# Memory attention of a perceiver stack on Trainium2: every probability block of a middle pair turned by VectorE and through DRAM, the second batch's transfers issued by ScalarE, and its weighting placed after the next pair's first scores

## What is computed

```python
def _L1_xattn_ref(x, memories, ln_g, ln_b, Wq, Wkv, Wm, Wo, bo):
    # HEADS = 16, DIM_HEAD = 64, INNER = 1024
    xn = (x - mu) * rsqrt(var + EPS) * ln_g + ln_b
    q = _split_heads(xn @ Wq)
    kv = xn @ Wkv
    k = _split_heads(kv[..., :INNER])
    v = _split_heads(kv[..., INNER:])
    mem = _split_heads(memories @ Wm)
    k = jnp.concatenate([k, mem], axis=2)
    v = jnp.concatenate([v, mem], axis=2)
    dots = jnp.einsum('bhid,bhjd->bhij', q, k) * DIM_HEAD ** (-0.5)
    attn = jax.nn.softmax(dots, axis=-1)
    out = jnp.einsum('bhij,bhjd->bhid', attn, v)
    return out.transpose(0, 2, 1, 3).reshape(b, n, h * d) @ Wo + bo
```

## Time and profile before

| | us |
|---|---|
| median of three runs | 2071.55 |
| range | 2068.11 to 2072.27 |
| the profiled execution's own time | 2070.35 |
| its span in the trace | 2068.6 |

### The profile page before, as it was taken

One profiled execution on the slowest core, in us unless ns is written; L12 is line 12 of the kernel. 1 busy time (PEld: TensorE's weight loads), 2 busy tenths in 40 slices (PEclk: granted clock), 3 DMA queues, 4 the chain that ended last, 5 costly groups with the idle time before them and its releaser, 6 DMA issues. The chain is left out here.

```text
span 2068.6 us, 34656 instructions
## 1 busy us (share of the span) xinstructions
PE 1985.6 (96%) x14206; PEld 1441.4 (70%) x14206; DVE 1229.0 (59%) x2068; ACT 882.2 (43%) x2075; POOL 61.1 (3%) x78
## 2 busy tenths in 40 slices
PE   7999999899999999989999999899999999989999
PEld 6864455578878888844446788677777777774687
DVE  6446589563356888899999310355444453548563
ACT  4224443353324323589997332233232332333342
POOL 0000000000000000200000000000000000000122
PEclk9999999999999999999999999899999999999999
DMA  7210000131110110120002145566567464643001
GB/s 267 82 49 1 1 2 2 42 107 41 41 42 21 62 42 25 58 102 1 21 1 94 52 139 166 169 181 172 130 185 187 116 191 126 160 159 100 1 1 41
DMA packets 125581, 174.73 MB, mean 84 GB/s; under 512 B 12256, under 2 KB 83936, under 8 KB 124960
## 3 DMA queue, kind: packets, MB, share of 16 engines
q1 hardware_dynamic: 125424, 172.52, 27.9%
HBM read 118.09 MB, written 22.94 MB: 68 GB/s over the span
## 5 line engine op out<-in xcount | busy, mean ns | idle before, releaser
L1307 ACT ACTIVATE R<-bank 128x512 f32<-128x512 f32 (+1 forms) x150 | 89.4, 599 | 393.2 <-PE bank L965 292.2
L1576 ACT ACTIVATE R<-R 128x64 f32<-128x64 f32 x896 | 217.0, 342 | 3.4 <-DVE R L2288 3.4
L962 PE MATMUL bank<-cth,wmh 128*128 128x512 f32 x512 | 207.4, 405 | 5.5 <-ACT arena L1681 4.2
L962 PE MATMUL bank<-cth,wml 128*128 128x512 f32 x512 | 200.7, 392 | 0.0
L532 PE MATMUL bank<-XN,arena 128*128 128x512 f32 x320 | 148.6, 617 | 0.0
L965 PE MATMUL bank<-ctl,wmh 128*128 128x512 f32 x512 | 137.8, 391 | 0.0
L962 PEld LDWEIGHTS bank<-cth,wmh 128*128 128x128 f32 x512 | 96.7, 189 | 39.3 <-issue 19.1
L532 PE MATMUL bank<-Y,arena 128*128 128x512 f32 x256 | 115.9, 597 | 1.7 <-ACT H L1619 1.7
L532 PEld LDWEIGHTS bank<-XN,arena 128*128 128x128 f32 x320 | 61.4, 198 | 72.1 <-issue 71.7
L965 PEld LDWEIGHTS bank<-ctl,wmh 128*128 128x128 f32 x512 | 96.6, 189 | 20.6
L962 PEld LDWEIGHTS bank<-cth,wml 128*128 128x128 f32 x512 | 96.8, 189 | 18.2
(11 more groups left out here) (442 smaller groups left out, 4173.9 us busy)
## 6 DMA issues: line engine op xcount, KB each, us to landing
Y<-value_turn SPq DMA_DIRECT2D x240, 128.0 KB, 2.9
H<-in_ctxT SPq DMA_DIRECT2D x30, 512.0 KB, 5.3
arena<-in_L_attn_mlp_w SPq DMA_DIRECT2D x8, 1024.0 KB, 5.2
probs<-R SPq DMA_DIRECT2D x15, 512.0 KB, 4.0
R<-probs SPq DMA_DIRECT2D x60, 128.0 KB, 3.1
R<-value_rows SPq DMA_DIRECT2D x32, 132.0 KB
arena<-in_L_ffn_Wg SPq DMA_DIRECT2D x4, 1024.0 KB, 6.7
arena<-in_L_ffn_Wu SPq DMA_DIRECT2D x4, 1024.0 KB, 5.3
```

The lines of the kernel that those rows point to most:

```text
L962: mm(bank, w_[:, o // 4, k, tl(o % 4)], cth[:, k, :, :], start=(k == 0 and w_ is wmh), stop=False)
L1307: fn(dst, src, ACT.Copy).then_inc(act_bank_free, 1)
L1576: last = fn(into[:, x // 2, h, :, x % 2], RC["Ey"][:, t, h, :], ACT.Copy, scale=RC["Ex"][:, t, h, 8 * j + x:8 * j + x + 1])
```

## The change

Pair 0 joins the last pair (`at_edge`): its values and probabilities go by TensorE alone, without transfers. In pairs 1 to 14 both batches' probabilities are turned by VectorE and sent through DRAM; b1 has its own DRAM buffer and semaphores, and its one transfer out and four back are issued by ScalarE among its copies. Unit 4 of the memories goes to a VectorE bank, as 2 and 3 do. `weighted(b1)` is issued by TensorE after the next pair's first scores, and VectorE scales its result after those scores' maxima. SyncE issues b0's four transfers back before the last four value transfers. The second scores come after units 2 and 3, and units 0 and 1 after them and unit 4.

```diff
+BY_DVE = (2, 3, 4)
...
+        def at_edge(pr):
+            return pr in (0, PAIRS - 1)
...
-                    b = open_dve(("mem", pr, o)) if o in (2, 3) else open_act(("mem", pr, o))
+                    b = open_dve(("mem", pr, o)) if o in BY_DVE else open_act(("mem", pr, o))
...
                 attention_scores(b0)
-                if pr == PAIRS - 1:
+                if pr:
+                    weighted(b0 - 1)
+                if at_edge(pr):
                     value_blocks(b0)
-                fill(2)
+                fill(2, 3)
+                attention_scores(b1)
+                if at_edge(pr):
+                    value_blocks(b1)
+                fill(4)
                 fill(0, 1)
                 if pr:
                     out_rows(pr - 1)
-                attention_scores(b1)
-                if pr == PAIRS - 1:
-                    value_blocks(b1)
-                fill(3)
                 if pr and pr % (CB // 2) == 0:
                     on_act(("ot", pr - 1))
                     output(pr // (CB // 2) - 1)
-                if pr == PAIRS - 1:
+                if at_edge(pr):
                     prob_blocks(b0)
-                fill(4)
-                prob_blocks(b1)
                 fill(5)
+                if at_edge(pr):
+                    prob_blocks(b1)
+                fill(6)
                 if pr == PAIRS - 1:
                     token_rows(4, 0)
                 prob_tail(pr)
-                fill(6, 7)
+                fill(7)
                 weighted(b0)
-                weighted(b1)
+            weighted(2 * PAIRS - 1)
...
                 exponentials(b0)
-                fill(0, 1)
+                exponentials(b1)
+                fill(0)
+                if not at_edge(pr):
+                    act.wait_ge(probs_turned[1], 2 * pr)
+                    if pr > 1:
+                        act.wait_ge(probs_full[1], 64 * (pr - 1))
+                    act.dma_start(dram["probs"][1].rearrange("c k j n -> (c k) (j n)"), prob_turn[1].rearrange("p j b n -> p (j b n)")
+                                  ).then_inc(probs_spilled[1], 16)
+                fill(1)
                 if pr:
                     out_rows(pr - 1)
-                exponentials(b1)
-                fill(4, 5, 6, 7)
+                fill(5)
+                if not at_edge(pr):
+                    act.wait_ge(probs_spilled[1], 16 * pr)
+                    for j in range(4):
+                        act.dma_start(probs_moved[1][32 * j:32 * j + 32].rearrange("p c b n -> p c (b n)"),
+                                      dram["probs"][1][:, :, j, :].rearrange("c k n -> k c n")).then_inc(probs_full[1], 16)
+                fill(6, 7)
...
                 maxima(b0)
-                if pr and pr + 1 < PAIRS:
-                    memory(pr + 1, (2,))
-                if pr < PAIRS - 1:
+                if pr:
+                    weighted(b0 - 1)
+                if at_edge(pr):
...
+                    values(b0)
+                else:
                     turn_values(pr)
-                    turn_probs(pr)
+                    memory(pr + 1)
+                maxima(b1)
+                if at_edge(pr):
+                    values(b1)
                 else:
...
-                maxima(b1)
-                if pr == PAIRS - 1:
-                    values(b1)
-                if pr and pr + 1 < PAIRS:
-                    memory(pr + 1, (3,))
+                    turn_probs(b0)
+                if pr + 1 < PAIRS:
+                    memory(pr + 1, (4,))
+                if not at_edge(pr):
+                    turn_probs(b1)
...
                 for a in range(4):
-                    if a == 2 and pr < PAIRS - 1:
...
+                    if a == 2:
+                        spill_probs(0)
+                    if a == 3:
+                        sp.wait_ge(probs_spilled[0], 16 * pr)
+                        for j in range(4):
+                            sp.dma_start(probs_moved[0][32 * j:32 * j + 32].rearrange("p c b n -> p c (b n)"),
+                                         dram["probs"][0][:, :, j, :].rearrange("c k n -> k c n")).then_inc(probs_full[0], 16)
                     for b in range(4):
                         sp.dma_start(RD["vt"][32 * b:32 * b + 32, :, a, :], value_turn[32 * a:32 * a + 32, :, b, :]
                                      ).then_inc(values_full, 16)
```

More of the change, by code:

```diff
@@ L247, in perceiver @@
         values_turned, values_full = sem("values_turned"), sem("values_full")
-        probs_turned, probs_spilled, probs_full = sem("probs_turned"), sem("probs_spilled"), sem("probs_full")
+        probs_turned, probs_spilled, probs_full = ([sem(f"{n_}{i}") for i in range(2)]
+                                                   for n_ in ("probs_turned", "probs_spilled", "probs_full"))
         k_full = [sem(f"k_full{i}") for i in range(2)]
@@ L390, in perceiver @@
         prob_turn = R[:, 14912:15936].rearrange("p (j b n) -> p j b n", j=4, b=2)
-        probs_moved = RD["pt"][:, 0:2, :].rearrange("p b n -> p (b n)").rearrange("p (c b n) -> p c b n", c=4, b=2)
+        two_moved = RD["pt"].rearrange("p (i b) n -> p i (b n)", i=2)
+        probs_moved = [two_moved[:, i].rearrange("p (c b n) -> p c b n", c=4, b=2) for i in range(2)]
+        prob_turn = [prob_turn, two_moved[:, 1].rearrange("p (j b n) -> p j b n", j=4, b=2)]
+        def at_edge(pr):
+            return pr in (0, PAIRS - 1)
         RDa = region([("p", (4, 612)), ("k", (2, 8, 64))], base=arena[:, 2:4, :, :].rearrange("p s a b -> p (s a b)"), limit=4096)
@@ L1070, in part @@
                     return last
-                if i == 0 and bb // 2 < PAIRS - 1:
-                    pe.wait_ge(values_full, 256 * (bb // 2 + 1))
-                if i == 0 and bb // 2 < PAIRS - 1:
-                    pe.wait_ge(probs_full, 64 * (bb // 2 + 1))
+                if not at_edge(bb // 2):
+                    pe.wait_ge(values_full, 256 * (bb // 2))
+                    pe.wait_ge(probs_full[i], 64 * (bb // 2))
                 for blk in range(2):
-                    if i:
-                        part(lambda g, c: RD["pt"][:, 2 + blk, 128 * g + 32 * c:128 * g + 32 * c + 32], RD["vt"][:, 2 + blk], blk == 0, None, False)
-                    else:
-                        part(lambda g, c: probs_moved[:, c, blk, 32 * g:32 * g + 32], RD["vt"][:, blk], blk == 0, None, False)
+                    part(lambda g, c: probs_moved[i][:, c, blk, 32 * g:32 * g + 32], RD["vt"][:, 2 * i + blk], blk == 0, None, False)
                 if i == 0:
@@ L1719, in _ @@
                     split_high(1)
-            memory(1, [o for o in EARLY if o not in (2, 3)])
+            memory(1, [o for o in EARLY if o not in BY_DVE])
             for pr in range(PAIRS):
```

71 lines of the change are left out of this document (33 added, 38 removed).

## The result

| kernel | median, us | range, us | runs |
|---|---|---|---|
| before | 2071.3 | 2065.96 to 2073.91 | 13 |
| after | 2082.82 | 2072.92 to 2085.98 | 13 |

The ratio is 1.0054 with a 95% interval of 1.0042 to 1.0066. The forecast was 2057 us with a range of 2049 to 2069, so time and sign are both wrong. Each ratio in this document is to launches of before made beside that kernel's own, and their medians lay between 2068.6 and 2071.3 us; where two kernels are a few us apart, read their ratios as well as their medians. The profiled execution of after took 2078.71 us; its span is 2076.9.

The account below looks back on a forecast made before the run. TensorE was taken as the bound. Pairs 0 to 14: 18.5 + 11 x 30.52 + 3 x 45.29 + 1.6 = 491.7 us against 507.07; 15.4 saved, less 1.0 in pair 15, gave 2057 us, range 2049 to 2069.

Parts of the forecast that it names:

- Pair 0: First pair, made without transfers: its weighting starts 18.5 us after the pair's start, where the pair took 29.46 us before.
- Rival 2: Pair 0 stays at half clock, so scores and a unit take 3.6 us more: 2061 us; chance 0.10.
- ScalarE's issues at nothing: ScalarE's five DMA issues of 0.5 us among its copies are covered by TensorE's work and cost nothing.
- Rival 3: ScalarE's issues and waits outrun their cover, unit 7 is emptied late and pairs grow; 2084 us at L = 2; chance 0.08.
- The chain to unit 0: Middle pairs: splits, maxima, turning, copies and first exponential hold TensorE 1.17 us before unit 0; the pair takes 30.41 us.
- Output pairs: Three pairs with output projection: 30.41 + 13.98 us plus a 0.90 us wait before `output` for ScalarE's copy, 45.29 us.
- Issuing: SyncE's 21 transfers per pair take 15.54 us to issue, plus some 0.3 us waiting for the trip to DRAM.
- The price of b1's trip: b1's 1.05 MB on the shared DMA engines delays the data by 0.9 us, from a possible 0 to 4.15.
- A wait before the weighting is not paid in full: Such a wait shortens the hold before unit 0, so data at 31.8 us give a middle pair of 30.52 us.
- Pair 15: Last pair gets b29's weighting behind its first scores; 1.0 us of the gain is given back there.
- Rival 1: Transfers collide: b1's trip costs 2 to 3.5 us, the weighting waits for values; 2066 us at 2.5; chance 0.22.

Follow-up runs that it names:

- e4: The kernel before with only pair 0 changed, its values and probabilities going by TensorE and VectorE without transfers; 2063.51 us.
- e10: e6 with a sixteenth of the bytes in each dummy transfer, same five issues and waits by ScalarE; 2060.29 us.
- e1: After, but b1's probabilities of pairs 1 to 14 are transposed by TensorE again and ScalarE issues no transfer; 2060.56 us.
- e5: e1 with VectorE taking the second maxima ahead of its two copies of memory units; 2050.76 us.
- e7: e1 plus dummy transfers with as many bytes as b1's trip, issued by SyncE behind the pair's last loads; 2064.84 us.
- e8: After, with ten extra matmuls of memory operands put into TensorE's waits before the weighting in pairs 1 to 12; 2075.45 us.
- e6: e1 plus ScalarE's five transfers at their old places as DRAM-to-DRAM dummies of b1's size that nobody uses; 2080.74 us.

## Why the prediction was wrong, by its own steps

- **Pair 0: right.** Forecast 20.1 us (18.5 and a weighting), measured 20.04, at a clock of 1.00. Rival 2 didn't come about. Of the 9.4 us by which pair 0 is shorter, 1.6 are the weighting moved out of it; the 7.7 us that e4 shows are its own.
- **ScalarE's issues at nothing: right.** The copies of units 6 and 7 are on time in after, and e10 has issues and waits at e1's time. Rival 3 is out.
- **The chain to unit 0: right in kind, too long.** Forecast 1.17 us of hold; e1 shows 0.6, e5 removes it and its pair is the unheld 30.03. In after it isn't seen at all, because TensorE is late at the weighting.
- **Output pairs: right in form.** The wait before `output` is there three times (2.2 us in all; 0.74 each, 0.90 forecast). The pairs take 44.1 us instead of 45.29, which is the hold that isn't there.
- **Issuing: right by luck.** SyncE's 21 issues took 1531.03 - 1515.58 = 15.45 us in pair 6 and 15.8 as the mean of the ten middle pairs after the first; 15.54 + 0.3 were forecast. But pair 6 has the longest issuing of these pairs in before, whose mean is 14.6, as in e1. So 1.2 us of what b1's trip costs lie here and were hidden by the choice of the pair.
- **The price of b1's trip: the step that failed.** I took 0.9 us, "nearest to the idle share". In pair 6 the last values landed 5.85 us after SyncE's last issue and not 2.9: with the 0.9 that is 2.05 us more than forecast. Pairs 5, 9 and 13 show it without anything else: no wait stands ahead of them, their values are turned at 12.12 us, as forecast (12.13), and their data are complete after 33.5 to 33.8 us, not 31.8. In e1, with the same turning, they are there after 30.7 or 30.8 at the latest. So b1's trip costs at least 2.8 us there. Three errors stand behind the early landing. The first is the base: 2.9 us is the median landing of all value transfers, while in before the weighting that waited for data came 2.8 to 4.1 us after the last issue (3.4 as a mean of seven pairs). Second, the idle share was read from one pair. These are the 20 us ahead of three weightings in before:

```profile
1490.01:1510.01 20.00, 19.82 (x121) 15.37 (x119) 8.14 (x15) 5.53 (x14) 0.76 (x2) 1.00 0.80 207
1521.09:1541.09 20.00, 19.38 (x119) 14.99 (x118) 7.39 (x14) 5.64 (x15) 0.77 (x2) 1.00 0.76 193
1551.10:1571.10 20.00, 19.69 (x120) 15.23 (x120) 8.28 (x15) 5.61 (x15) 0.76 (x2) 1.00 0.82 211
```

  The earlier trace rows is from the middle one, the emptiest of the three. Third, a mean over 19 us says nothing about when the idle time comes: ScalarE's reads fell on SyncE's last four transfers, and from there on the engines were full. e7 shows that as many bytes behind these transfers cost 4 us, not 20.
- **"A wait before the weighting is not paid in full": right behind short waits, failed behind the long ones.** The argument was that the first maxima hang on the splits, at 5.31 us after TensorE is ready, so that a wait delays nothing. Behind five waits of 1.51 to 2.56 us they began at 5.24 to 5.42 us, behind two of 1.95 and 2.08 us with slow matmuls after them at 5.72 and 5.96. Behind the four waits of over 3 us they began at 7.07 to 7.75, since they also need the scores, which stand behind the weighting. In pair 6 TensorE was ready at 1504.67 - 3.69 = 1500.98 and the maxima began at 1508.48, 7.50 us later. 3.81 us of this lie between weighting and maxima; at full clock, behind the first filled wait of e8, these are 1363.86 - 1361.55 = 2.31. So of the 2.19 us by which the maxima are late, 1.50 are the clock's, and by this estimate only 0.69 would have been passed on without it. The first maxima behind the wait of 1.99 us in after, and those of e8:

```profile
1540.14 0.81 DVE L2449 TENSOR_REDUCE small<-bank 128x1 f32<-128x289 f32 x2
```

```profile
1363.86 0.82 DVE L2452 TENSOR_REDUCE small<-bank 128x1 f32<-128x289 f32 x2
```

  With 0.25 us more up to the end of turning, the values of pair 6 were turned at 1515.55, 14.57 us after the start and not 12.13. The sum for this pair: 31.8 + 2.44 (turning) - 0.39 (issues) + 2.05 (landing) = 35.90 us, and the data were complete at 1536.88 - 1500.98 = 35.90. As a mean of the ten pairs it is 31.8 + 1.0 - 0.1 + 2.0 = 34.7 us. The forecast also halved the waits of pairs 1, 5, 9 and 13, which have no wait ahead of them that could shorten theirs; three of them are 3.56 to 3.72 us.
- **A term that was missing: the clock.** The forecast knew of the half clock in pair 0 alone. Behind each wait of over 3 us in the middle pairs it fell as well, and lengthened the time from the weighting to the scores by 0.8 to 1.0 us (2.30 to 2.51 against 1.51), ahead of the maxima. e8 puts what follows from it at some 14 us.
- **Pair 15: too small.** From its first scores to line 1175 pass 48.7 us, 44.4 before (line 1168 there), so 4.3 are given back and not 1.0. Every kernel of the study has it, at 48.0 to 51.3 us, e4 too, where the weighting wasn't moved. A wait of 1 to 4 us among the 32 small matmuls behind the last weightings, for which the profile names no releaser, stands in all of them but was 0.47 in before. Its cause wasn't tried.

The balance of the profiled executions, after against forecast: middle pairs 11 x (33.08 - 30.52) = +28.2; output pairs 132.2 - 135.9 = -3.6; pair 15 +3.3; ahead of pair 0 -5.0, which is an execution's chance. Together +22.9, and 2078.71 - 2055.95 = 22.8.

**The rivals.** Rival 1 named the mechanism, with the right place and sign to look for ("the weighting waiting over 1 us for the values' transfers"), and its price of 2 to 3.5 us holds the 2.95 us that pair 6 shows in its landing (5.85 - 2.9), and the 2.8 us or more against e1. It gave 2066 us for 2.5, and 2075 for all 4.15. At 2.95 its own formula gives (30.9 + 2.95 + 29.24)/2 = 31.55 us a pair; the 33.08 measured are 1.53 more, 17 us in eleven pairs: the clock, what the long waits pass on, and the four waits that nothing halves. It had a chance of 0.22. The range's lower end doesn't follow from the forecast's own sum: with nothing paid for the transfers the chain's 30.41 us would set the pair, 0.11 less than 30.52, which is 1.2 us in eleven pairs and not the 8 down to 2049.

The Trainium skill, "DMA: Bandwidth & Descriptors", section "Issuing engines are not separate DMA queues", says that transfers started by different engines interleave on the same hardware and that a second issuer saves issue time alone. The runs agree: e6 costs 20 us with bytes that nobody uses, e10 nothing with as many issues. I cited it and then priced the trip near the other end.

## What to carry to other kernels

Price added transfers by what they do to the landing of the consumer's last transfer, over several iterations, not by a mean idle share or by full engines alone; and if they have slack of their own, start them behind the transfers that have none (e6 against e7: 16 us for the same bytes). Before halving a wait, follow it once around the loop, at the clock that stands behind it: here the long waits, with the fallen clock, delayed scores, maxima, turning and so the next transfers. When a kernel loses to a wait, first remove the suspected traffic and keep the rest of the change: here the rest of the change was no loss (e1), and the order of two steps that was worth nothing in it was worth ten microseconds without that traffic.

## What was not expected of the hardware

- Added traffic from a second issuer had no price at 0.5 MB a pair (2059.3 us) and 20 us at 1.05 MB (2080.7). Without any (e1) the value transfers landed within 4.6 us at most (median 3.1), with b1's trip within 7.1 (median 3.4): the median hardly tells, the last transfers do.
- A wait of 3.69 us in after lowered the mean granted clock to 0.57 over the next 2 us. At about 2 us it went either way: in after the 64 matmuls of the weighting took 1.10 us behind waits of 1.99, 2.34 and 2.56 us, but 1.69 and 1.92 behind waits of 1.95 and 2.08; behind one of 2.01 in e6 they took 1.93, at a clock of 0.51 in the 2 us after it. Ten matmuls in the waits kept the mean clock of the 14 pairs at 1.00, and the program with 29 us more of TensorE's work was 7 us faster by the medians, 5 by the ratios.
